# One more wait of GpSimd in the gathers of two edge attentions

## The reference

```python
score = sum(q[dst] * k[src]) ...            # per edge and head
m     = segment_max(score, dst)
ex    = exp(score - m[dst])
denom = segment_sum(ex, dst)
agg   = segment_sum((ex / denom[dst]) * v[src], dst)
```

## Time and profile before

| | us |
|---|---|
| runs | 6724.58, 6731.64, 6753.25 |
| median | 6731.64 |
| span of the profiled execution | 6706.8 |
| median less span | 24.8 |
| POOL gathers of `l0e` and `l3e`, busy | 986.1 and 971.0 |

### The profile page before, as it was taken

How to read it: one execution, slowest core, us unless ns; L and a number is a source line. 1 busy time by engine, 2 the same in 40 slices (tenths; PEclk the granted TensorE clock), 3 DMA queues, 4 the chain that set the end, 5 groups by cost and what they waited for, 6 DMA issues and landing times. The chain is left out here.

```text
span 6706.8 us, 90264 instructions
## 1 busy us (share of the span) xinstructions
PE 4342.6 (65%) x24913; PEld 3150.9 (47%) x24913; DVE 3458.5 (52%) x6689; ACT 2184.9 (33%) x7656; POOL 3192.9 (48%) x3187
## 2 busy tenths in 40 slices
PE   6996676766677744544444546887646666666676
PEld 4664454544445423333333435766335555555553
DVE  4452666666666662211111231112558888888885
ACT  1221455555545430000000111222225454555541
POOL 0422566666666236676676520002145565655551
PEclk8896777777777876666766778998778888888885
DMA  4334666666666525333333407882366666666673
GB/s 133 126 123 163 182 197 199 202 196 198 198 196 197 125 72 186 93 93 93 92 95 92 72 29 243 261 262 87 108 189 205 203 210 203 205 207 203 201 185 102
DMA packets 509932, 1077.03 MB, mean 161 GB/s; under 512 B 94770, under 2 KB 322388, under 8 KB 505993
## 3 DMA queue, kind: packets, MB, share of 16 engines
q0 software_dynamic: 204144, 617.42, 32.6%
q1 hardware_dynamic: 296854, 452.03, 20.2%
q10 hardware_dynamic: 8512, 2.74, 0.2%
HBM read 964.49 MB, written 194.54 MB: 173 GB/s over the span
## 5 line engine op out<-in xcount | busy, mean ns | idle before, releaser
L772 POOL DMA_INDIRECT l0e_kv<-t_table,k_recs x912 | 986.1, 1081 | 636.9 <-ACT l0e_vw L1049 375.5
L772 POOL DMA_INDIRECT l3e_kv<-t_table,k_recs x912 | 971.0, 1065 | 667.5 <-ACT l3e_vw L1049 368.0
L1464 PE MATMUL l2e_pA<-l2e_row,l2e_oh 128*128 128x257 f32 x1824 | 633.4, 516 | 768.7 <-issue 380.4
L1418 POOL DMA_INDIRECT l2e_row<-t_table,l2e_idx x912 | 899.7, 986 | 389.7 <-issue 265.4
L1464 PEld LDWEIGHTS l2e_pA<-l2e_row,l2e_oh 128*128 128x128 f32 x1824 | 460.0, 262 | 942.0 <-issue 852.9
L1006 PE MATMUL l0e_pA<-l0e_vw,l0e_ohf 128*128 128x260 f32 x1824 | 643.9, 500 | 198.3 <-ACT l0e_vw L1049 129.2
L958 PE MATMUL l3e_pQE<-l3e_qb,l3e_ohT 128*128 128x256 bf16 x2736 | 428.0, 318 | 405.9 <-issue 378.7
L1049 ACT ACTIVATE l3e_vw<-l3e_kv,l3e_w 128x64 f32<-128x64 f32 x2736 | 679.8, 334 | 0.0
L1049 ACT ACTIVATE l0e_vw<-l0e_kv,l0e_w 128x64 f32<-128x64 f32 x2736 | 679.6, 334 | 0.0
L1443 DVE SCALAR_TENSOR_TENSOR l2e_acc<-l2e_acc,k_itf,l2e_pA 128x257 f32<-128x257 f32 x228 | 109.9, 482 | 1058.6 <-issue 981.9
L1006 PEld LDWEIGHTS l0e_pA<-l0e_vw,l0e_ohf 128*128 128x128 f32 x1824 | 427.7, 247 | 338.5 <-ACT l0e_vw L1049 156.6
(11 more groups left out here) (469 smaller groups left out, 7126.8 us busy)
## 6 DMA issues: line engine op xcount, KB each, us to landing
exp_w<-in_L_gnn_w SPq DMA_DIRECT2D x224, 512.0 KB
t_table<-l0n_tab SPq DMA_DIRECT2D x26, 2048.0 KB, 6.9
l0e_qb<-t_q SPq DMA_DIRECT2D x228, 192.0 KB
l3e_qb<-t_q SPq DMA_DIRECT2D x228, 192.0 KB
t_agg<-l0e_acc SPq DMA_DIRECT2D x228, 130.0 KB
t_agg<-l3e_acc SPq DMA_DIRECT2D x228, 130.0 KB
l0e_drow<-t_drow SPq DMA_DIRECT2D x57, 512.0 KB
l3e_drow<-t_drow SPq DMA_DIRECT2D x57, 512.0 KB
```

The costliest lines, as they stand in the source:

```text
L772: pool.indirect_dma_start(kv[:, n % SK, g, :], None, table[:, :], bass.IndirectOffsetOnAxis(ap=K["recs"][:, n, g, ridx:ridx + 1], axis=0)) ...
L1418: pool.indirect_dma_start(row[:, s, g, 0:D], None, table[:, :], bass.IndirectOffsetOnAxis(ap=idx[:, i, g:g + 1], axis=0)).then_inc(row_rea ...
L1464: last = pe.matmul(pA[s % 2][:, 0:W], oh[:, s, g, :], row[:, s, g, :], start=(g == 0), stop=(g == G - 1))
```

## The change

In front of the gathers of an item `n` with `n % 4 == 1`, from item 9 on, POOL also waits for `sh_ps`:

```diff
                 if n >= SK:
                     pool.wait_ge(vwa_ready, n - SK + 1)
                     pool.wait_ge(vwd_ready, n - SK + 1)
+                if n % BI == 1 and n > 2 * BI:
+                    pool.wait_ge(sh_ps, (n - 1) // BI - 1)
                 for g in range(G):
                     pool.indirect_dma_start(kv[:, n % SK, g, :], ...
```

## The result

The kernel after is slower: 7084.5 us in place of 6731.0 (medians of four runs each), a ratio of 1.0513 with a 95% interval of 1.0483 to 1.0543. The forecast was 6605 us, with a range from 6485 to 6770. The profiled spans are 7096.6 and 6706.8 us, 389.8 apart. By the first and last instruction of each stage, `l0e` went from 1661.5 to 1781.0 us (+119.5) and `l3e` from 1685.6 to 1956.2 (+270.6); all else together is within 1 us.

The account below looks back on a forecast made before the run. The prediction took a ring in l0e, where gathers hold PE's shift and so z, as the bound. Saving 127 us there and nothing in l3e gave 6731.6 - 127 = 6605 us, range 6485 to 6770.

Parts of the forecast that it names:

- The hold: In l0e, others see PE's results only when POOL's gathers run out; z came 8.1 us after the shift's recorded end.
- The rival that it has another cause: In l0e, z's 8.1 us delay is not the gathers' doing: 6731 us, up to 6780; no change by two causes 0.19.
- z will follow the shift: In l0e, z should come less than 4 us after the shift's record, about 2 us after POOL's twelfth gather.
- 24.55 us for a four: In l0e, z to z without slow fours: 24.55 us in place of 28.28, 3.73 less.
- that fits if the chain stays as it is: In l0e, the chain from z to shift takes 20.55 us, and POOL's stop comes at about 22.5.
- A third of the fours is slow, held at the turned ends: In l0e, a third of fours take 28.7 us, the rest 24.55: mean 25.9, 127 us less over 53 fours.
- one odd four: In l0e, after an early z, the turned ends' copy waited 4.85 us; the next z came 27.55 us later.
- the rival's point at 70% slow fours: In l0e, the case of a slower kernel decides when more than 0.7 of the fours are slow.
- the sign that I had named: L1057's wait for the turned ends (L979) at 4 us or more in most fours would show the slower case.
- l3e at nothing, 55 us either way: In l3e, moved gathers fit 2.34 us of idle time, cost nothing; DVE's wait ahead of L814 could add or save 55.
- L814's wait: In l3e, DVE's wait ahead of L814, 55.1 us in 47 waits, could double or go.
- The slower rival: Turned ends held in most fours: 20 to 80 us more in l0e, up to 55 in l3e, about 6800; chance 0.19.

Follow-up runs that it names:

- m3: Six orders of POOL's waits, nine fours each, in one kernel, against before, on a chip with the hold: 6907.9 us beside 6757.8.
- m4: Orders of before and after with gather rows of 2048, 1024 and 512 bytes in one kernel, against before, with the hold: 6871.0 us, before 6697.6.
- e1: Against before: POOL's new wait for the shift in l0e alone, l3e unchanged, on a chip without the hold: 6069.0 us, ratio 1.0007.
- order 4: Segment with the shift's wait ahead of the last item's third gather, against before's order: l0e four 25.1 us (28.6), l3e 28.9 (29.6).
- e12: Against before: shift's wait ahead of the third gather of each burst's last item, both stages, with the hold: 6530.3 us to 6713.0, ratio 0.9729.
- e5: After plus a wait for DVE's products ahead of the next burst, both stages, with the hold: 6969.7 us, ratio 1.0296 to before.

## Why the prediction was wrong, point by point

- *The hold is tied to the gathers*: right, and shown: by the order alone in m3, and by the stages that differ between chips. The rival that it has another cause falls. Too simple was that what PE has done is seen only when the gathers have run out: before's own trace has a result 10.5 us into a burst that passes at once. That the hold is a property of some chips could not be read from one trace.
- *z will follow the shift*: right (0.81 us in place of 8.1); POOL's wait ahead of the last item, forecast at 2 to 3 us, is 3.3 on average. Nearly none was forecast elsewhere, but POOL waits for DVE's weighting as well, 6.8 us in a four, since that stands behind the held products.
- *24.55 us for a four*: wrong. The step that failed is the sentence "that fits if the chain stays as it is". I carried the 20.55 us from z to the shift over from an order in which POOL was idle for the first 4.36 us of it. I had priced that idle time as room for the last item's gathers, and as nothing else. It was also the time in which DVE came to see PE's queries for the steps behind z.
- *A third of the fours is slow, held at the turned ends*: the kind was right, place and share were wrong. I took the place from one odd four and asked only about that place. The held step was the queries at 1819.07, 4.1 us into the new run, and DVE waited so ahead of their product in 48 fours of some 50. With the rival's point at 70% slow fours, that alone turns the sign. By the sign that I had named, ACT's wait for the turned ends at 4 us or more, it would not have been found: that wait is 2.9 us at most. I laid the new run of gathers against the one step that had been seen to suffer, not against each step of PE behind z. That would have named the queries as a risk, no more: before lets results through later in a run than these.
- *l3e at nothing, 55 us either way*: the term that was mis-sized most: 270.6 us. I costed the four gathers that move and not the run that they make with the eight behind them, 5374.56 to 5389.84. I did name L814's wait; its line went from 55.1 us in 47 waits to 391.1 in 62 (between 5080 and 6900 us).
- *The slower rival* at 6800 was the right one in kind, with a chance of 0.19; its price (20 to 135 us) was well under half of the real one (353), because it had a slow four of `l0e` at 28.7 to 29.8 us (30.5 measured) and gave `l3e` 55 us at most. The range ended at 6770 and so did not even hold it whole.
- *The rule of the Trainium skill* ("SBUF — State Buffer", "SBUF: two separate sides": engine and DMA ports are disjoint, PE never waits there). By it there would have been no change, and that did not come. m4 agrees with its first half: 110 GB/s less traffic leave a four as long as it was. What the traces with the hold show lies behind the matmuls: their semaphores rise late. The rule and the hold can both be true if the hold is not in SBUF; no run shows where it is. Nor do they tell whether a held result was really complete at its recorded end, which is modelled.

## What to carry to other kernels

When a wait moves work of one engine, lay the new run of that work against every result that others need in that time, not only against the one that is to be freed. Idle time that looks free may be what lets the others through. Ask of each rest in a ring who uses it before you fill it: here, on chips with the hold, two gathers in it gained 2.7%, and four cost 5%. And take a second chip before you tune to a delay that no instruction explains: on seven of ten the whole effect, gain and loss, was not there.

## What the runs showed of the hardware

On some chips results of PE are seen late by DVE, ACT and POOL while POOL issues indirect DMAs without a pause: 11.65 us for the queries that were over on record at 1819.07, 8.1 for the shift before. The late part is the rise of PE's semaphore (1830.62 for these queries). In the traces of the seven other chips the shift's semaphore in `l0e` rises 0.01 to 0.02 us behind its recorded end, and e1 shows z 0.04 us behind the shift.

How far into a run of gathers a result comes does not tell whether it is held. Queries 3.1 us in passed at once (m3's order 4: over at 1856.71, in a run from 1853.60), and so did the turned ends of before 10.5 us in (1530.73, from 1520.26). Queries 4.1 us in did not (after: 1819.07, from 1814.97), and the result behind before's turned ends was held for 2.5 us, though the run went on. Holds of shifts ended in rests of POOL of 1.7 to 2.9 us (e12, e5).

With the hold the kernel before takes some 11% longer (6731 against 6065 us), nearly all of it in `l0e`, `l2e` and `l3e`. A quarter of the bytes changes nothing about it. The page's clock and busy shares don't name it; a wait for "remote", or for a releaser long done, is how it looks.
